# First stage of a four-stage graph kernel: the second bias of group 1 is summed on GpSimd, the gates of group 2 move up, more constant products on TensorE

## The chip, the cores and the metric

The kernel runs on one core of a Trainium2 chip. The metric is the device time of one execution in microseconds (us); lower is better. The engines are named as the profile does: PE (TensorE) with PEld (its weight loads), DVE (VectorE), ACT (ScalarE), POOL (GpSimd), SP (SyncE, which issues the DMAs).

## What is computed

`x` is 32 batches of 256 nodes with 128 features, `adj` a 256x256 matrix, all in float32. Four layers follow each other, each of them `x = layernorm(x + L(x))`. The change lies in the first:

```python
def _L0_gnn_ref(x, adj_in, adj_out, bias_in, bias_out, ...):
    msg_in = (einsum('nm,bmd->bnd', adj_in, x) + bias_in) * sigmoid(x @ gate_w_in + gate_b_in)
    msg_out = (einsum('nm,bmd->bnd', adj_out, x) + bias_out) * sigmoid(x @ gate_w_out + gate_b_out)
    msg_loop = x * sigmoid(x @ loop_gate)
    return relu(msg_in + msg_out + msg_loop)
```

Both adjacency matrices are the same `adj` here. With the gates g0, g1, g2 (one number per node and batch) the sum is `(adj x)(g0+g1) + bias_in g0 + bias_out g1 + x g2`. The later layers are a graph convolution with two batch norms, an attention layer, and a graph layer with ten LSTM steps; they are not touched.

## The kernel before

The 32 batches are worked on in `GROUPS` = 8 groups of `GB` = 4. A group is 8 tiles (`TILES`) of 128 nodes by 128 features, ordered as two halves (`NC` = 2) of four. Every engine has an instruction list of its own, written by hand, and the lists meet only in semaphores (`wait_ge`, `then_inc`), so the order of the statements in each engine's function is the order of its work.

The work of one group g in the first stage is this.

- PE: `gates(g)` (L574) gives the gates' sums, `neighbours(g)` (L582) gives `adj x`. Group 1 writes its neighbour sums to its own PSUM tile (named QQ in the profile), all others to PB. After the layer norm, `spread(g)` (L596) and `widen(g)` (L610) begin the second layer.
- DVE: `gate_sum(g)` (L1203) adds the gate biases. `gate_out(g)` (L1211 writes GG, L1213 writes GS = g0+g1) follows ACT's tanh. `mix(g)` makes the sum: eight L1284 (neighbour sum times GS, plus the tile V), eight L1291 (plus x times g2), for some groups one L1298 over all 1024 columns (plus the tile V2), one L1302 (relu, plus x), eight L1248 (statistics), then six small instructions L1260 to L1270 that end in the variance VAR.
- ACT: `squash(g)` (L940) is the tanh, `first_bias(g)` (L947) writes `V = bias_in g0` in eight instructions, `norm_apply` (L935) writes the normed tiles X.
- POOL: `second(g)` (L437) writes `V2 = bias_out g1` in two instructions, `both_biases(g)` (L446) adds V2 to V in two, and `rstd` (L413, L419) turns VAR into the scale RSD and the offset OFF for which `norm_apply` waits.

`APART` (L341) is the number of groups at the beginning whose V2 is added by DVE (L1298) and not by POOL (L446). It is 2 before: groups 0 and 1. In POOL's list `second(1)` stands behind `rstd(0, ...)` of group 0 and straight in front of `second(2)`. On PE, `spin(bank, count)` (L544) issues products of the constant tile `ones` whose results nobody reads: 8 of them before the first `neighbours(0)`, 10 before `spread(0)`.

Of the kernel before, what the change touches and what calls it, by code (L numbers as in the profile page):

```python
# [24 lines left out]
P = 128  # L25
BATCH, NODES, FEAT = 32, 256, 128
NC = NODES // P
GB = 4
# [62 lines left out]
def build(nc, x, xt, adj, early_in, later_in, lstm_w, out):  # L91
    ctx = ExitStack()
    with ctx:
# [6 lines left out]
        def reach(eng, s, n):  # L100

            if isinstance(n, int) and n <= 0:
                return
            eng.wait_ge(s, n)
# [94 lines left out]
        Q = [QQ[:, k * BANK:(k + 1) * BANK] for k in range(4)]  # L199
# [114 lines left out]
        def halves(g, h):  # L314
            return 2 * g + (2 if h is None else h + 1)

        def size(h):
            return 2 if h is None else 1
# [7 lines left out]
        def tls(h):  # L326
            return slice(0, TILES) if h is None else slice(h * TILES // 2, (h + 1) * TILES // 2)

        def nth(buf, t):
            return buf[:, t * P:(t + 1) * P]  # L330


        def near(g):
            return QA if g == 1 else PB
# [3 lines left out]
            return min(n, GROUPS)  # L338


        APART = 2  # L341


        NCHUNK, AHEAD = 2 * GROUPS, 3
# [55 lines left out]
        def _(pool):  # L400
# [7 lines left out]
            def rstd(k, kk, g, h=None):  # L408

                n, some = (halves(g, h), size(h)) if k in (1, 2) else (g + 1, 1)  # L410
                ts = tls(h)
                pool.wait_ge(ln[k]["var"], n)
                pool.tensor_tensor(RSD[kk][:, ts], VAR[kk][:, ts], pw[:, ts], ALU.pow).then_inc(ln[k]["rstd"], some)  # L413
                if k in (0, 1) or (k == 3 and g == GROUPS - 1):
                    pool.wait_ge(ln[k]["mean"], n)
                    pool.wait_ge(ln[k]["rstd"], n)
                    if k == 0:
                        reach(pool, ln[k]["out"], TILES * (g - 1))
                    pool.tensor_tensor(OFF[kk][:, ts], MEAN[kk][:, ts], RSD[kk][:, ts], ALU.mult).then_inc(ln[k]["off"], some)  # L419

            def wide(k):
                return BIO[:, k].unsqueeze(2).broadcast_to([P, NC, GB, P])

            def gate(g, k):
                return GG[g % 2][:, :, k:k + 1].rearrange("p (c b) q -> p c b q", c=NC).broadcast_to([P, NC, GB, P])

            def by_tile(buf):
                return buf.rearrange("p (c b d) -> p c b d", c=NC, b=GB)


            def second(g):

                pool.wait_ge(gate_g, g + 1)
                reach(pool, mix2, min(g - 1, APART))
                reach(pool, both_ok, NC * (g - 1 - APART))
                for c in range(NC):
                    pool.tensor_tensor(by_tile(V2[g % 2][:])[:, c:c + 1], wide(1)[:, c:c + 1], gate(g, 1)[:, c:c + 1],  # L437
                                       ALU.mult).then_inc(second_ok, 1)
# [13 lines left out]
            for c in range(NC):  # L452
                s = slice(c * P, (c + 1) * P)
                pool.wait_ge(norm_ok, NC + c + 1)
                pool.tensor_tensor(AN[:, c, s], AN[:, c, s], DIAG[:, c, :], ALU.add).then_inc(diag_ok, 1)
            rstd(0, 0, 0)
            second(1)
            for g in range(APART, GROUPS + 1):
                if g < GROUPS:
                    second(g)  # L460
# [79 lines left out]
        def _(pe):  # L540

            def spin(bank, count):
                for _ in range(count):
                    pe.matmul(bank, ones[:], ones[:], start=True, stop=True)  # L544
# [22 lines left out]
            def gates(g):  # L567
                pe.wait_ge(xt_in[g % NX], 16 * (g // NX + 1))
                if g == 0:
                    pe.wait_ge(early_ok, 16)  # L570
                reach(pe, gate_z, g)
                for c, b in ORDER:
                    at = (c * GB + b) * 4
                    mm = pe.matmul(Q[3][:, at:at + 4], turned(XT[:, g % NX], c, b), GW, start=True, stop=True)  # L574
                mm.then_inc(gate_ps, 1)
# [35 lines left out]
                              start=True, stop=True).then_inc(hid_ps, 1)  # L611

            pe.wait_ge(zero_ok, 1)
            spin(Q[0][:, 0:P], 8)
            pe.wait_ge(adjt_in, 16)
            neighbours(0)
            gates(0)
# [2 lines left out]
            neighbours(2)  # L620
            turn_adj()
            gates(2)
            spin(Q[2][:, 0:P], 10)
            for g in range(1, GROUPS + 1):
                spread(g - 1)
                if g + 2 < GROUPS:
# [163 lines left out]
            def lstm_x(g, par, k):  # L790

                p, s, _, nw = STEPS[k]
                if k == 0:
                    pe.wait_ge(h1_ok, 2 * (g + 1))
                    pe.wait_ge(z2_ok, TILES * 2) if g == 0 else None
                elif s == 0 and p > 1:
                    pe.wait_ge(h_ok, NSTEP * g + LAST_BEFORE[p] + 1)
                for q in gates_of(k):

                    before = max((j for (kk, qq), j in GATE_AT.items() if qq == q and kk < k), default=None)  # L800
                    last = max(j for (kk, qq), j in GATE_AT.items() if qq == q)
                    reach(pe, g_ok, NGATE * g + before + 1 if before is not None else NGATE * (g - 1) + last + 1)
                    mm = pe.matmul(steps_view(Q[q], k), WT[:, 0, (p - 1) * 4 + q, :], ht_view(par, k),  # L803
                                   start=True, stop=(s == 0))
                    if s == 0:
                        mm.then_inc(g_ps, 1)
# [382 lines left out]
        def _(dve):  # L1189
# [8 lines left out]
            def gate_sum(g):  # L1198
                dve.wait_ge(gate_ps, g + 1)
                if g == 0:  # L1200
                    dve.wait_ge(early_ok, 16)
                reach(dve, gate_t, g)
                dve.tensor_tensor(GZ[:].rearrange("p t q -> p (t q)"), Q[3][:, 0:TILES * 4],  # L1203
                                  GBI, ALU.add).then_inc(gate_z, 1)

            def gate_out(g):
                dve.wait_ge(gate_t, g + 1)
                reach(dve, first_ok, TILES * (g - 1))
                reach(dve, second_ok, NC * (g - 1))
                reach(dve, loop_ok, TILES * (g - 1))  # L1210
                dve.tensor_scalar(GG[g % 2][:], GT[:], 0.5, 0.5, ALU.mult, ALU.add).then_inc(gate_g, 1)  # L1211
                dve.wait_ge(gate_g, g + 1)
                dve.tensor_tensor(GS[g % 2][:], GG[g % 2][:, :, 0], GG[g % 2][:, :, 1], ALU.add).then_inc(gate_s, 1)  # L1213
# [36 lines left out]
            def norm_stats(k, kk, z, g, h=None):  # L1250

                norm_tiles(k, kk, z, g, h)
                norm_small(k, kk, g, h)
# [18 lines left out]
            def mix(g):  # L1272
                z = ZS[g % 2]
                if g == 1:
                    gate_sum(2)
                dve.wait_ge(gate_s, g + 1)
                dve.wait_ge(agg0_ps, g + 1)
                reach(dve, ln[0]["out"], TILES * (g - 1))
                for t in range(TILES):
                    if g < APART:  # L1280
                        dve.wait_ge(first_ok, TILES * g + t + 1)
                    elif t % GB == 0:
                        dve.wait_ge(both_ok, NC * (g - APART) + t // GB + 1)
                    dve.scalar_tensor_tensor(out=nth(z, t), in0=nth(near(g), t), scalar=GS[g % 2][:, t:t + 1],  # L1284
                                             in1=nth(V[g % 2], t), op0=ALU.mult, op1=ALU.add).then_inc(mix1, 1)
                if g == 1:
                    gate_out(2)
                dve.wait_ge(x_in[g % NX], 16 * (g // NX + 1))
                dve.wait_ge(mix1, TILES * (g + 1))
                for t in range(TILES):  # L1290
                    dve.scalar_tensor_tensor(out=nth(z, t), in0=nth(XIN[:, g % NX], t), scalar=GG[g % 2][:, t, 2:3],  # L1291
                                             in1=nth(z, t), op0=ALU.mult, op1=ALU.add).then_inc(loop_ok, 1)
                if g == 0:
                    gate_sum(1)
                dve.wait_ge(loop_ok, TILES * (g + 1))
                if g < APART:
                    dve.wait_ge(second_ok, NC * (g + 1))
                    dve.tensor_tensor(z[:], z[:], V2[g % 2][:], ALU.add).then_inc(mix2, 1)  # L1298
                    dve.wait_ge(mix2, g + 1)
                if g == 0:  # L1300
                    gate_out(1)
                dve.scalar_tensor_tensor(out=z[:], in0=z[:], scalar=0.0, in1=XIN[:, g % NX], op0=ALU.max,  # L1302
                                         op1=ALU.add).then_inc(mix3, 1)
                dve.wait_ge(mix3, g + 1)
                norm_stats(0, g % 2, z, g)
# [383 lines left out]
            g = GROUPS - 1  # L1689
# [53 lines left out]
```

## Time and profile before

| | us |
|---|---|
| three runs | 669.52, 670.06, 670.72 |
| their median | 670.06 |
| the profiled execution | 672.63 |
| its span on the core | 670.8 |
| busy in the span: PE, DVE, ACT, POOL | 635.3, 484.4, 426.6, 209.6 |

The span runs from the first to the last instruction in the trace, and 1.8 us of the profiled execution lie around it. The first stage, on which the change works, takes the first 110 us or so. Times of instructions below are counted from the start of the span. "<-" behind an idle time names what ended it.

### The profile page before, as it was taken

Reading aid. Unit: us, or ns where it says so; the run is one execution under the profiler, and the core shown is the slowest. Engines: PE = TensorE matmul, PEld = TensorE weight load, DVE = VectorE, ACT = ScalarE, POOL = GpSimd, SP = SyncE. Lnnn points to the kernel's source line nnn. Section 1 sums busy time; section 2 is a strip of 40 time slices with the busy share of each in tenths; the row PEclk is TensorE's granted clock in tenths of the full one; section 3 lists DMA queues with packets and bytes.
Section 4 is the critical chain, followed back from the end, with each engine's and each line's share of the span. In section 5 each row is a group of like instructions: output and inputs, shape, how many; then the busy total and the mean of one; then the engine's idle time right before and its main releaser. Section 6 shows DMA issues by size and latency. Waiting matters only on the chain.

```text
span 670.8 us, 9346 instructions
## 1 busy us (share of the span) xinstructions
PE 635.3 (95%) x2666; PEld 436.2 (65%) x2666; DVE 484.4 (72%) x1616; ACT 426.6 (64%) x953; POOL 209.6 (31%) x261
## 2 busy tenths in 40 slices
PE   9879999998899999999999999999999999999993
PEld 5745656446785687578657757765785686677573
DVE  3999999877856657876876787688668756465355
ACT  2656767866747665775667567656857666456562
POOL 2545451005724123234406132450522243012031
PEclk9989999998799999999999999999999999999998
DMA  8234000000000000000000000000000000000000
GB/s 330 108 110 173 1 1 1 1 0 1 0 1 1 0 1 0 1 0 33 1 0 19 13 1 0 33 1 0 1 31 1 0 33 0 1 1 32 1 32 31
DMA packets 4371, 16.82 MB, mean 25 GB/s; under 512 B 480, under 2 KB 480, under 8 KB 4192
## 3 DMA queue, kind: packets, MB, share of 16 engines
q1 hardware_dynamic: 4320, 16.23, 6.3%
q8 instruction: 21, 0.34, 0.2%
q14 instruction: 30, 0.25, 0.1%
HBM read 12.03 MB, written 4.19 MB: 24 GB/s over the span
## 4 chain that ended last, share of the span: by engine, by line
PE 63%; DVE 12%; ACT 6%; issue 3%; POOL 1%; DVEq 0%; ACTq 0%; POOLq 0%
PE QQ L803 22%; PE QQ L815 14%; PE PA L758 4%; PE PA L786 3%; PE PB L777 2%; PE PB L640 2%; PE PA L640 2%; DVE HT L1522 2%; ACT raw L1089 2%; ACT HB L1052 2%; DVE raw L1544 2%; PE PB L739 1%; PE PA L739 1%; PE PA L596 1%; ACT raw L1101 1%
## 5 line engine op out<-in xcount | busy, mean ns | idle before, releaser
L1089 ACT ACTIVATE raw<-QQ,BL 128x256 f32<-128x256 f32 (+4 forms) x312 | 166.6, 557 | 96.1 <-PE QQ L815 52.0
L803 PE MATMUL QQ<-HT,WT 128*128 128x256 f32 (+2 forms) x624 | 205.8, 473 | 6.7 <-ACT raw L1089 3.7
L803 PEld LDWEIGHTS QQ<-HT,WT 128*128 128x128 f32 x624 | 115.5, 190 | 73.9 <-issue 30.9
L413 POOL TENSOR_TENSOR RSD<-VAR,pw 128x8 f32<-128x8 f32 (+1 forms) x42 | 61.2, 1458 | 239.6 <-DVE VAR L1270 239.6
L815 PE MATMUL QQ<-HB,WT 128*128 128x256 f32 (+2 forms) x384 | 114.5, 441 | 2.0 <-DVE HB L1562 1.6
L815 PEld LDWEIGHTS QQ<-HB,WT 128*128 128x128 f32 x384 | 70.1, 190 | 36.1 <-issue 15.3
L500 POOL TENSOR_TENSOR HB<-HB 128x512 f32<-128x512 f32 x28 | 35.1, 1274 | 133.8 <-ACT HB L1042 133.8
L1101 ACT ACTIVATE raw<-raw 128x256 f32<-128x256 f32 (+4 forms) x88 | 41.5, 472 | 40.9 <-DVE raw L1544 32.5
L1534 DVE SCALAR_TENSOR_TENSOR raw<-raw 128x512 f32<-128x512 f32 (+2 forms) x66 | 39.4, 597 | 28.0 <-ACT raw L1089 27.4
L1562 DVE SCALAR_TENSOR_TENSOR HB<-raw 128x256 f32<-128x256 f32 (+4 forms) x48 | 21.8, 455 | 23.3 <-ACT raw L1101 23.3
L610 PE MATMUL QQ<-one_b,later 128*128 128x512 f32 x64 | 30.2, 613 | 4.7 <-ACT HB L974 4.5
L935 ACT ACTIVATE X<-Z,OFF,RSD 128x128 f32<-128x128 f32 x80 | 31.8, 481 | 2.0 <-POOL OFF L419 2.0
L481 POOL TENSOR_SCALAR X<-four,MEAN,RSD 128x128 f32<-128x128 f32 x64 | 32.4, 519 | 1.6
L596 PE MATMUL PA<-AHT,X 128*128 128x256 f32 x128 | 30.2, 390 | 1.9 <-ACT X L935 1.9
L1052 ACT ACTIVATE HB<-HB,EB 128x256 f32<-128x256 f32 x64 | 30.7, 495 | 1.6 <-POOL HB L500 1.5
L1562 DVE SCALAR_TENSOR_TENSOR HT<-raw 128x512 f32<-128x512 f32 (+4 forms) x40 | 21.7, 544 | 12.8 <-ACT raw L1101 12.4
L596 PEld LDWEIGHTS PA<-AHT,X 128*128 128x128 f32 x128 | 24.2, 194 | 10.2 <-issue 6.9
L758 PE MATMUL PA<-AD,X 128*128 128x256 f32 x128 | 30.5, 381 | 0.0
L786 PE MATMUL PA<-AD,Y 128*128 128x256 f32 x128 | 29.3, 381 | 0.0
L582 PE MATMUL PB<-four,AD 128*128 128x512 f32 x56 | 28.0, 647 | 0.6 <-DMA four<-in_x 0.6
L492 POOL TENSOR_SCALAR four<-HB,MEAN,RSD 128x128 f32<-128x128 f32 x56 | 28.1, 518 | 0.7
L758 PEld LDWEIGHTS PA<-AD,X 128*128 128x128 f32 x128 | 24.1, 193 | 6.4 <-issue 3.8
(223 smaller groups left out, 1101.0 us busy)
## 6 DMA issues: line engine op xcount, KB each, us to landing
four<-in_x SPq DMA_DIRECT2D x8, 512.0 KB, 3.7
raw<-in_xt SPq DMA_DIRECT2D x8, 512.0 KB, 6.4
out<-four SPq DMA_DIRECT2D x7, 512.0 KB, 2.7
WT<-in_lstm SPq DMA_DIRECT2D x1, 2048.0 KB, 9.3
later<-in_later SPq DMA_DIRECT2D x1, 725.5 KB, 10.0
AD<-in_adj SPq DMA_DIRECT2D x2, 256.0 KB, 4.9
out<-four SPq DMA_DIRECT2D x2, 256.0 KB, 2.0
early<-in_early SPq DMA_DIRECT2D x1, 275.0 KB, 4.4
```

The source lines that it names most:

```text
L413: pool.tensor_tensor(RSD[kk][:, ts], VAR[kk][:, ts], pw[:, ts], ALU.pow).then_inc(ln[k]["rstd"], some)
L500: pool.tensor_tensor(f.E1[:, 2 * b:2 * b + 2], f.E2[:, 2 * b:2 * b + 2], f.MS[:, 2 * b:2 * b + 2], ALU.add).then_inc(e_ok, 1)
L596: mm = pe.matmul(PA[:, b * NODES:(b + 1) * NODES], tile_of(X1, g, m, b), AHT[:, m, :], start=(m == 0), stop=(m == NC - 1))
L758: mm = pe.matmul(PA[:, b * NODES:(b + 1) * NODES], tile_of(X1, g, m, b), ADJT[:, m, :], start=(m == 0), stop=(m == NC - 1))
L786: mm = pe.matmul(PA[:, b * NODES:(b + 1) * NODES], turned(Y, m, b), ADJT[:, m, :], start=(m == 0), stop=(m == NC - 1))
L803: mm = pe.matmul(steps_view(Q[q], k), WT[:, 0, (p - 1) * 4 + q, :], ht_view(par, k), start=True, stop=(s == 0))
L815: pe.matmul(Q[q][:, 0:nw * GB], WT[:, 1, (p - 1) * 4 + q, :], HS[:, (k - 1) % 2, 0:nw * GB], start=False, stop=True).then_inc(g_ps, 1)
L1052: e = act.activation(f.E1[:, t], f.E1[:, t], ACT.Exp, bias=f.EB[:, t:t + 1], scale=SLOPE, accum_out=DEN[:, t:t + 1] if g > 1 else None)
L1089: act.activation(TG[q][:, at:n], Q[q][:, at:n], ACT.Tanh, scale=0.5 if q == G else 0.25, bias=BL[:, p - 1, q:q + 1]).then_inc(g_ok, 1)
L1101: act.activation(TC[:, at:n], CELL[:, at:n], ACT.Tanh, scale=0.5).then_inc(tc_ok, 1)
L1534: dve.scalar_tensor_tensor(out=target[:, 0:n], in0=TG[I][:, 0:n], scalar=1.0, in1=TG[G][:, 0:n], op0=ALU.add, op1=ALU.mult).then_inc(cell_ ...
L1562: dve.scalar_tensor_tensor(out=to[:, at:nw], in0=steps_view(TG[O], k)[:, at:nw], scalar=1.0, in1=steps_view(TC, k)[:, at:nw], op0=ALU.add, ...
```

## The change

```diff
-        APART = 2
+        APART = 1
...
@@ POOL's list
                 pool.wait_ge(norm_ok, NC + c + 1)
                 pool.tensor_tensor(AN[:, c, s], AN[:, c, s], DIAG[:, c, :], ALU.add).then_inc(diag_ok, 1)
-            rstd(0, 0, 0)
-            second(1)
             for g in range(APART, GROUPS + 1):
                 if g < GROUPS:
                     second(g)
                     both_biases(g)
                 rstd(0, (g - 1) % 2, g - 1)
...
@@ PE's list
             pe.wait_ge(zero_ok, 1)
-            spin(Q[0][:, 0:P], 8)
+            spin(Q[0][:, 0:P], 10)
...
             gates(2)
-            spin(Q[2][:, 0:P], 10)
+            spin(Q[2][:, 0:P], 20)
...
@@ DVE's mix(g)
                     dve.scalar_tensor_tensor(out=nth(z, t), in0=nth(near(g), t), scalar=GS[g % 2][:, t:t + 1],
                                              in1=nth(V[g % 2], t), op0=ALU.mult, op1=ALU.add).then_inc(mix1, 1)
-                if g == 1:
-                    gate_out(2)
+                    if (g, t) == (1, GB - 1):
+                        gate_out(2)
```

POOL's order at the beginning of the first stage, the difference between the two kernels. HT and Y are the two V2 tiles (group 1 has HT, group 2 has Y), one_a is V of group 1.

```order
 L455 TENSOR_TENSOR HB<-HB 128x128 [waits norm_ok] x2
+L437 TENSOR_TENSOR HT<-early,GG 128x512 [waits gate_g]
+L437 TENSOR_TENSOR HT<-early,GG 128x512
+L446 TENSOR_TENSOR one_a<-one_a,HT 128x512 [waits second_ok,first_ok] x2
 L413 TENSOR_TENSOR RSD<-VAR,pw 128x8 [waits ln0_var]
 L419 TENSOR_TENSOR OFF<-MEAN,RSD 128x8 [waits ln0_rstd,ln0_mean]
-L437 TENSOR_TENSOR HT<-early,GG 128x512 [waits gate_g]
-L437 TENSOR_TENSOR HT<-early,GG 128x512
 L437 TENSOR_TENSOR Y<-early,GG 128x512 [waits mix2,gate_g]
```

The two L437 of group 1 have moved in front of the L413 and L419 of group 0, and two L446 of group 1 are new behind them.

DVE's order in the mix of group 1, before:

```order
L1284 SCALAR_TENSOR_TENSOR X<-QQ,GS,one_a 128x128 [waits first_ok,agg0_ps,gate_s]
L1284 SCALAR_TENSOR_TENSOR X<-QQ,GS,one_a 128x128 [waits first_ok] x7
L1211 TENSOR_SCALAR GG<-GT 128x32 [waits second_ok,loop_ok,first_ok,gate_t]
L1213 TENSOR_TENSOR GS<-GG 128x8 [waits gate_g]
L1291 SCALAR_TENSOR_TENSOR X<-four,GG,X 128x128 [waits mix1,x_in1]
L1291 SCALAR_TENSOR_TENSOR X<-four,GG,X 128x128 x7
L1298 TENSOR_TENSOR X<-X,HT 128x1024 [waits second_ok,loop_ok]
L1302 SCALAR_TENSOR_TENSOR X<-X,four 128x1024 [waits mix2]
```

and now (the lines of the changed kernel are smaller by two from here on):

```order
L1282 SCALAR_TENSOR_TENSOR X<-QQ,GS,one_a 128x128 [waits both_ok,agg0_ps,gate_s]
L1282 SCALAR_TENSOR_TENSOR X<-QQ,GS,one_a 128x128 x3
L1209 TENSOR_SCALAR GG<-GT 128x32 [waits second_ok,loop_ok,first_ok,gate_t]
L1211 TENSOR_TENSOR GS<-GG 128x8 [waits gate_g]
L1282 SCALAR_TENSOR_TENSOR X<-QQ,GS,one_a 128x128 [waits both_ok]
L1282 SCALAR_TENSOR_TENSOR X<-QQ,GS,one_a 128x128 x3
L1289 SCALAR_TENSOR_TENSOR X<-four,GG,X 128x128 [waits mix1,x_in1]
L1289 SCALAR_TENSOR_TENSOR X<-four,GG,X 128x128 x7
L1300 SCALAR_TENSOR_TENSOR X<-X,four 128x1024 [waits loop_ok]
```

The 1024-column addition of V2 is gone, the first four and the last four sums now wait for POOL's `both_ok`, and the gates GG and GS of group 2 stand in the middle of the eight.

## Rows read from the trace of the kernel before

**Rows 1.** Busy time by stretch: us, busy (instructions) of each engine, PEclk, DMA share, GB/s

```profile
24.00:40.90 16.90, 10.66 (x60) 8.27 (x60) 16.24 (x46) 7.71 (x22) 9.64 (x9) 1.00 0.28 108
40.90:44.30 3.40, 3.19 (x5) 1.42 (x6) 3.30 (x11) 2.62 (x8) 2.83 (x4) 0.50 0.07 28
44.30:103.00 58.70, 58.55 (x222) 36.49 (x221) 56.73 (x185) 41.99 (x107) 29.98 (x28) 1.00 0.16 64
```

**Rows 2.** Waits of DVE and of PE from 24 to 110 us: total, times, longest

```profile
DVE Z L1284 <- DVE GS L1213: 0.4, 1, 0.4
DVE GG L1211 <- ACT GT L940: 0.3, 1, 0.3
...
PE QQ L610 <- ACT HB L974: 4.5, 1, 4.5
```

**Rows 3.** Timeline, PE at the start of spread(6): start, us busy, what, [idle before it]

```profile
103.00 3.69 PE L596 MATMUL PA<-AHT,X 128*128 128x256 f32 x16 [0.15 <-ACT X L935]
```

**Rows 4.** Timeline of DVE and POOL, the mix of group 1

```profile
24.63 0.17 DVE L1270 TENSOR_SCALAR VAR<-SQD 128x8 f32<-128x8 f32 x1
...
24.86 2.16 DVE L1284 SCALAR_TENSOR_TENSOR X<-QQ,GS,one_a 128x128 f32<-128x128 f32 x8
...
26.83 2.05 POOL L437 TENSOR_TENSOR HT<-early,GG 128x512 f32<-128x512 f32 x2
...
26.93 0.98 DVE L1211 TENSOR_SCALAR GG<-GT 128x32 f32<-128x32 f32 x1
...
28.84 5.86 DVE L1291 SCALAR_TENSOR_TENSOR X<-four,GG,X 128x128 f32<-128x128 f32 x8
28.84 2.10 POOL L437 TENSOR_TENSOR Y<-early,GG 128x512 f32<-128x512 f32 x2
...
31.34 2.68 POOL L446 TENSOR_TENSOR one_d<-one_d,Y 128x512 f32<-128x512 f32 x2 [0.40 <-ACT one_d L947]
...
34.73 1.22 DVE L1298 TENSOR_TENSOR X<-X,HT 128x1024 f32<-128x1024 f32 x1
...
39.62 0.17 DVE L1270 TENSOR_SCALAR VAR<-SQD 128x8 f32<-128x8 f32 x1
```

**Rows 5.** Timeline of DVE and POOL, the mix of group 3

```profile
53.29 2.16 DVE L1284 SCALAR_TENSOR_TENSOR X<-PB,GS,one_a 128x128 f32<-128x128 f32 x8
...
55.55 2.19 DVE L1291 SCALAR_TENSOR_TENSOR X<-four,GG,X 128x128 f32<-128x128 f32 x8
...
59.03 1.65 DVE L1248 BATCH_NORM_STATS2 STL<-X 128x6 f32<-128x128 f32 x8
...
60.15 2.52 POOL L446 TENSOR_TENSOR one_d<-one_d,Y 128x512 f32<-128x512 f32 x2 [4.95 <-ACT one_d L947]
60.71 0.74 DVE L1260 TENSOR_TENSOR SUM<-STL 128x16 f32<-128x16 f32 x1
...
61.57 1.13 DVE L1263 TENSOR_TENSOR SQD<-DIF 128x8 f32<-128x8 f32 x1
...
62.93 0.17 DVE L1270 TENSOR_SCALAR VAR<-SQD 128x8 f32<-128x8 f32 x1
```

**Rows 6.** Timeline of DVE and POOL, the end of group 0

```profile
20.70 0.18 DVE L1211 TENSOR_SCALAR GG<-GT 128x32 f32<-128x32 f32 x1
...
21.00 1.22 DVE L1302 SCALAR_TENSOR_TENSOR Z<-Z,four 128x1024 f32<-128x1024 f32 x1
...
24.88 1.65 POOL L413 TENSOR_TENSOR RSD<-VAR,pw 128x8 f32<-128x8 f32 x1 [6.41 <-DVE VAR L1270]
```

**Rows 7.** Timeline of PE and DVE, the first 17 us

```profile
1.03 3.78 PE L544 MATMUL QQ<-ones 128*128 128x128 f32 x16 [1.03 <-DVE ones L1215]
...
5.43 6.03 PE L582 MATMUL PB<-four,AD 128*128 128x512 f32 x8 [0.62 <-DMA four<-in_x]
...
13.00 3.68 PE L582 MATMUL QQ<-four,AD 128*128 128x512 f32 x8
...
13.18 0.19 DVE L1203 TENSOR_TENSOR GZ<-QQ,early 128x32 f32<-128x32 f32 x1 [3.03 <-PE QQ L574]
```

## The prediction

> **What bounds the kernel now.** I read the busy time by stretch first, then the waits, then the timeline of the groups around the change. The busy time [rows 1] shows two engines that are almost never idle in the first stage: from 24.0 to 40.9 us DVE is busy for 16.24 of 16.90 us while PE works only 10.66; from 44.3 to 103.0 DVE is busy for 56.73 of 58.70 us and PE for 58.55. The waits [rows 2] say the same: between 24 and 110 us DVE waits twice, for 0.3 and 0.4 us. PE has one long wait in that stretch, 4.5 us for ACT in widen(0), and ACT there is itself waiting for a gate sum that DVE issues late. So the first stage goes at DVE's pace, with PE just behind. At spread(6) the two meet: PE waits 0.15 us for a normed tile [rows 3], which comes out of DVE's variance. Whatever DVE gains before 103 us moves the rest of the program, if PE follows; the later stages are untouched.
>
> DVE's "busy" is not all work. Eight L1291 take 2.19 us in group 3 [rows 5] and 5.86 us in group 1 [rows 4]; GG takes 0.98 us in group 1 and 0.18 in the group before [rows 6]. In group 1 POOL's L437, L437 and L446 (2.05, 2.10 and 2.68 us) run just beside these. L1284 (2.16 us in both groups) and L1248 (1.65) do not stretch beside POOL: L437 starts at 26.83 while L1284 ends, and L446 at 60.15 runs beside L1248. The Trainium skill (SBUF — State Buffer, "Who interferes with whom") has the rule: a DVE instruction with two SBUF inputs contends with a GpSimd instruction that reads SBUF, and the second one to come blocks fully. By that rule the trace agrees: L1291, L1298, L1302 and the small L1260 to L1267 mostly have two such inputs, L1284 and L1248 have one. The change is therefore mostly about which DVE instruction stands beside POOL's.
>
> **Part 1: group 0 gets slower.** POOL's four instructions of group 1 now start when GG of group 1 is ready, 20.88 us (20.70 + 0.18) [rows 6], in what was an idle time of 6.41 us in front of L413. They are 2.05 us (two L437, rows 4) and 2.52 us (two L446, rows 5), together 4.6 us. Beside them DVE has L1302, which starts at 21.00, the eight L1248, and the small ones. Either L1302 is held behind the first L437, by about what GG lost in group 1, 0.98 - 0.18 = 0.8 us, or it goes first and POOL's four end that much later. The L446 meet the small ones as in group 3, where L1260 took 0.74 and L1263 1.13 us [rows 5]; undisturbed ones take 0.17, so that costs 1.5 us. Together the variance of group 0 comes **2.3 us later**. Bounds: 0, if every piece of POOL's falls beside L1248 or waits, and 4.6 us, if all of it stops DVE. I take 2.3, since group 3 shows the same L446 pair at the same place. POOL's four are through by then (20.9 + 4.6 = 25.5, or some 26.7 if L1302 goes first, against a variance at 26.9), so L413, and the new wait of L1284 for both_ok, cost nothing more; the cover for that is a few tenths. What is queued behind the new wait for first_ok on POOL is L413 itself, and ACT's first bias of group 1 starts at the same GG, so it keeps ahead.
>
> **Part 2: the mix of group 1 gets faster.** Before, it takes from L1284 at 24.86 to VAR at 39.62, 14.76 us [rows 4]. The new one is made from group 3 [rows 5], which has no L1298 either: 5.74 us from L1284 to L1248 (53.29 to 59.03), 1.68 to L1260, and from L1260 to VAR 2.22 less the 1.5 us of blocking, 0.7. That is 8.1 us. GG and GS in the middle of the L1284 add 0.4, but no longer meet an L437: those wait for GG and for L419 of group 0. L437 starts 1.97 us after the first L1284 (26.83 against 24.86), and that distance stays, since both hang on VAR of group 0; the pair then ends 4.0 us after it. L1291 begins at 2.26 + 0.4 = 2.7, so it is held for about 1.2 us. Before, two pairs stood there, HT and Y; now only Y. The L446 of group 2 hang on ACT's first bias and would start 31.34 - 24.86 = 6.5 us after the first L1284. DVE is then in L1302 (6.1 plus the 1.2 of blocking, less the 1.2 it takes, to 8.5 at the latest), so POOL is the one held, or L1302 is; L1248 shields DVE after that, and the end of the second L446 costs the small ones 0.8. Sum: 8.1 + 0.4 + 1.2 + 0.8 = 10.5 us, **4.3 us less than 14.76**. It contains the L1298 removed (1.22 us) and the rest is blocking that goes. Less the 2.3 of part 1, DVE is ahead by **2.0 us** after group 1. With the bounds of part 1 that term lies between -0.3 and +4.3.
>
> From group 2 on the lists are as before, and hang on the same chain. PE has to follow: spread(1) hangs on VAR of group 1 and so moves with it. PE also loses less to its clock. Before, its 4.5 us wait is followed by a stretch from 40.9 to 44.3 us with a granted clock of 0.5, the 1.2 GHz level [rows 1, 2]; now widen(0) has its ACT copy about 2 us earlier, while spread(0) ends 2.3 us later, so the gap shrinks to nearly nothing, and a matmul stream that ran at 1.2 GHz for part of those 3.4 us may run at 2.4. That puts PE ahead of DVE and not behind, so I count nothing for it. The twelve extra products cost PE: ten of them, at half of the 0.47 us (3.78 / 8) that one takes in the first stretch [rows 7], 2.4 us. They fill the 2.3 us by which the normed tiles of group 0 are late, and behind them PE has that 4.5 us wait as a reserve. Nothing.
>
> **Part 3: the first products.** At the start PE's four neighbour products of group 0 take 6.03 us, those of group 1 3.68 [rows 7]. It is the same work: the first ran mostly at 1.2 GHz, the second at 2.4. Before the first, PE had been busy from 1.03 to 4.81 and idle for 0.62. DVE's first gate sum waits for PE at 13.18, so this is on the path. Two more products are 0.9 us and close the gap; then PE is busy without a break from 1.03 instead of 5.43, and the clock can rise before or in the neighbour products. Bounds: 6.03 - 3.68 = 2.35 us if they run wholly at 2.4 GHz; 0.3 us lost (0.9 - 0.6) if the rise comes where it came before and the extra products are in the way. I take **2.0 us**, near the upper end, because the break is the only thing between two busy stretches and 4.4 us of busy time are added in front. The Trainium skill (TensorE: Matmul & The Clock Gate, Part 1) says that the place of the rise varies between runs of the same kernel, with where the first matmul falls. By that rule this term would be an average and could not be read from one trace; the three runs before spread over 1.2 us, which would fit. No trace here shows it.
>
> **Sum.** 2.0 + 2.0 = 4.0 us off the profiled execution's 672.63. The median of the runs is 670.06, 2.6 us lower; I take the same saving from it: **666.1 us**. A measurement of this kernel can tell about 0.2%, 1.3 us, from no change.
>
> **The rivals.**
> - The forecast, both terms as above: 666.1. Chance 0.48.
> - The clock does not rise earlier. For it: between 1.03 and 4.81 PE was already busy and the level did not change. Only part 1 and 2 count: 670.06 - 2.0 = 668.1. Chance 0.21.
> - POOL blocks DVE in full in group 0 (4.6 us instead of 2.3), and only the clock helps: 670.06 + 0.3 - 2.0 = 668.4. For it: in group 1 three pairs of POOL's cost DVE 3.7 us in L1291 (5.86 - 2.19) and 0.8 in GG [rows 4], most of their length. Against it: 1.65 us of DVE's time there is L1248. Chance 0.09.
> - Neither helps, or the one eats the other; that is also the case in which the change does not do what it says: 669.7 to 670.4. Chance 0.13.
> - Slower: L446 comes to stand beside L1291. In group 1 that cost about 2 us (of the 3.7 in L1291), in group 3 the same L446 costs 1.5 beside L1260 to L1263, and where it meets only one small one less than 1. If the normed tiles and the first biases of ACT come earlier against DVE in groups 3 to 7, by more than the 1.1 us between the start of L1248 and of L446 (59.03 and 60.15) plus L1302's 1.2, then each of the five groups pays about 1 us more: +5.0 - 2.0 = 3.0 over, 673.1 without the clock's help. Against it: ACT's first bias hangs on PE, and PE gains at most the 1.7 us of the slow clock over DVE. Chance 0.09.
>
> **How the numbers follow.** Faster by over 0.2% are the first three, 0.78; within 0.2% the fourth, 0.13; slower 0.09. The range goes from 663.4, where part 1 costs 0.5 and the clock gives 2.3 (4.3 - 0.5 + 2.35 is 6.2; 663.9, and some tenths for PE's clock), to 669.0, beyond the second and third cases.
>
> **What the profile would show.** Right: L1302 and the small instructions of group 0 stretched, VAR of group 0 some 2.3 us later against its gate sum; no L1298 in group 1, L1291 there near 3.4 us and no longer 5.86; GG of group 2 near 0.18; L1284 to VAR in group 1 near 10.5; PE's wait in widen(0) gone and no 0.5 clock around 41 us; the neighbour products of group 0 near 3.9 us and the first gate sum near 11.2. Wrong, if the first gate sum still comes at 13.2, if L1284 of group 1 waits for both_ok, or if PE starts to wait for ACT in groups 3 to 7.

## The result, and the profile after

The changed kernel takes 664.18 us (median of five runs, 662.84 to 665.25) against 670.06 us (five runs, 668.51 to 673.05): a ratio of 0.9908, 95% interval 0.9885 to 0.9931. That is 5.9 us less, where 4.0 were forecast, and it lies inside the range.

The profiled executions differ by more, 661.2 against 670.8 us of span. To see why, the trace needs one marker in the middle. The start of spread(6), the matmul group that waited for DVE in [rows 3], serves well: it is near the end of the first stage, and behind it the two programs are the same.

The timeline of the changed kernel, PE and DVE at the start (its lines are smaller by two; start, us busy, what), against [rows 7]:

```profile
1.03 4.52 PE L542 MATMUL QQ<-ones 128*128 128x128 f32 x20 [1.03 <-DVE ones L1213]
...
5.47 3.67 PE L580 MATMUL PB<-four,AD 128*128 128x512 f32 x8
...
10.86 0.19 DVE L1201 TENSOR_TENSOR GZ<-QQ,early 128x32 f32<-128x32 f32 x1 [1.58 <-PE QQ L572]
```

The four neighbour products of group 0 take 3.67 us in place of 6.03, and the first gate sum comes at 10.86 instead of 13.18. Which clock level such a short stretch had is read here from the durations, since the granted-clock column shows 1.00 at the start of both traces, while the same four products take 6.03 or 3.67 us. Where the rise falls can be read too: the instructions of the constant products start 0.21 us apart before it and 0.11 us behind it, those of the neighbour products take 1.06 and then 0.59 us. In the kernel before it comes at 10.2 us, in the changed one at 5.3.

The same view, the end of group 0 on DVE and POOL, against [rows 6]:

```profile
18.64 3.04 POOL L437 TENSOR_TENSOR HT<-early,GG 128x512 f32<-128x512 f32 x2 [2.49 <-DVE GG L1209]
18.68 2.08 DVE L1300 SCALAR_TENSOR_TENSOR Z<-Z,four 128x1024 f32<-128x1024 f32 x1
...
21.64 2.51 POOL L446 TENSOR_TENSOR one_a<-one_a,HT 128x512 f32<-128x512 f32 x2
22.48 0.45 DVE L1258 TENSOR_TENSOR SUM<-STL 128x16 f32<-128x16 f32 x1
...
23.05 1.13 DVE L1261 TENSOR_TENSOR SQD<-DIF 128x8 f32<-128x8 f32 x1
...
24.41 0.17 DVE L1268 TENSOR_SCALAR VAR<-SQD 128x8 f32<-128x8 f32 x1
```

L437 and L1300 start 0.04 us apart and hold each other: L1300 takes 2.08 us for 1.22, and the two L437 take 3.04 for 2.05, since the second is held while L1300 runs. The L446 then hold L1258 and L1261.

And the mix of group 1, against [rows 4]:

```profile
24.64 1.13 DVE L1282 SCALAR_TENSOR_TENSOR X<-QQ,GS,one_a 128x128 f32<-128x128 f32 x4
...
25.68 0.17 DVE L1209 TENSOR_SCALAR GG<-GT 128x32 f32<-128x32 f32 x1
...
26.62 2.10 POOL L437 TENSOR_TENSOR Y<-early,GG 128x512 f32<-128x512 f32 x2
...
27.20 3.24 DVE L1289 SCALAR_TENSOR_TENSOR X<-four,GG,X 128x128 f32<-128x128 f32 x8
...
30.48 1.23 DVE L1300 SCALAR_TENSOR_TENSOR X<-X,four 128x1024 f32<-128x1024 f32 x1
...
31.12 2.94 POOL L446 TENSOR_TENSOR one_d<-one_d,Y 128x512 f32<-128x512 f32 x2 [2.40 <-ACT one_d L945]
...
34.61 0.17 DVE L1268 TENSOR_SCALAR VAR<-SQD 128x8 f32<-128x8 f32 x1
```

L1289 takes 3.24 us in place of 5.86, GG 0.17 in place of 0.98, L1298 is gone, and the L446 of group 2 now meet L1300, where POOL is the one that waits (2.94 us in place of 2.52). The last two rows are PE at spread(1) and spread(6), against [rows 3]:

```profile
37.91 3.69 PE L594 MATMUL PA<-AHT,X 128*128 128x256 f32 x16 [0.97 <-ACT X L933]
...
97.30 3.69 PE L594 MATMUL PA<-AHT,X 128*128 128x256 f32 x16 [0.15 <-ACT X L933]
```

spread(6) starts at 97.30 against 103.00, 5.7 us earlier. So the first stage carries what the medians show. The other 3.9 us of the two spans come later, 2.6 of them by 224 us, behind the stretch of the attention stage where the clock differs. Busy time by stretch, the kernel before (the column behind the five engines is the granted clock; 1.00 is 2.4 GHz and 0.50 is 1.2 GHz):

```profile
163.80:177.40 13.60, 11.47 (x78) 9.02 (x77) 11.92 (x57) 12.13 (x30) 8.02 (x7) 1.00 0.00 1
177.40:184.30 6.90, 6.31 (x29) 5.86 (x28) 4.81 (x21) 3.96 (x10) 5.31 (x7) 0.51 0.00 0
```

and the changed kernel:

```profile
155.00:158.40 3.40, 3.40 (x10) 1.74 (x9) 1.47 (x8) 3.40 (x10) 3.26 (x4) 0.57 0.00 0
158.40:653.00 494.60, 479.56 (x2098) 340.18 (x2096) 342.81 (x1175) 320.26 (x712) 150.04 (x192) 1.00 0.02 8
```

Each trace has one fall of 3.4 us near 155 to 160 us. The trace of before has 6.9 us more at the 1.2 GHz level from 177.4 on, the other none. The length of that second fall differs from one execution of the same kernel to the next, as the repeated traces below show, and a version of the changed kernel has it too (`after_10_10`, 6.8 us at a granted clock of 0.50 from 172.3 on). So I don't count it as the change's work. It is not shown that the change has no part in it: the fall is in all three traces of the kernel before.

### The profile page after: what moved, and what is told of

Its sections match the earlier page's. It is cut to its first block, busy times and chain, and to the rows that moved or that the text cites. A ratio compares the mean times of both kernels' runs of the same rounds, so it can differ in the third digit from the quotient of the medians.

```text
span 661.2 us, 9396 instructions
## 1 busy us (share of the span) xinstructions
PE 630.9 (95%) x2690; PEld 434.8 (66%) x2690; DVE 481.7 (73%) x1615; ACT 426.9 (65%) x953; POOL 214.4 (32%) x263
## 4 chain that ended last, share of the span: by engine, by line
PE 64%; DVE 11%; ACT 6%; issue 3%; POOL 1%; DVEq 0%; ACTq 0%; POOLq 0%
PE QQ L801 23%; PE QQ L813 14%; PE PA L756 4%; PE PA L784 4%; PE PB L775 2%; PE PB L638 2%; PE PA L638 2%; DVE HT L1520 2%; ACT HB L1050 2%; ACT raw L1087 2%; DVE raw L1542 1%; PE PB L737 1%; PE PB L823 1%; PE PA L737 1%; DVE HB L1435 1%
## 5 line engine op out<-in xcount | busy, mean ns | idle before, releaser
L413 POOL TENSOR_TENSOR RSD<-VAR,pw 128x8 f32<-128x8 f32 (+1 forms) x42 | 61.7, 1470 | 223.9 <-DVE VAR L1268 223.9
L784 PEld LDWEIGHTS PA<-AD,Y 128*128 128x128 f32 x128 | 24.2, 190 | 5.0 <-DVE Y L1513 0.7
```

The source lines that it names most:

```text
L784: mm = pe.matmul(PA[:, b * NODES:(b + 1) * NODES], turned(Y, m, b), ADJT[:, m, :], start=(m == 0), stop=(m == NC - 1))
```

## The experiments

In the table below, "gate sum" is the start of DVE's first GZ and "spread(6)" the start of PE's eight products of that group, both from the timeline of each profiled execution. Times are in us. Each is a median, and the ratio is to runs of the kernel before on the same chip (its medians there were 669.97, 669.83, 668.97 and 669.86 us). Two versions that ran on different chips are compared best by their ratios; 0.001 is 0.67 us.

| kernel | time | ratio, interval | neighbours(0) | gate sum | spread(6) | from one to the other |
|---|---|---|---|---|---|---|
| before | 670.06 | | 6.03 | 13.18 | 103.00 | 89.82 |
| changed | 664.18 | 0.9908, 0.9885 to 0.9931 | 3.67 | 10.86 | 97.30 | 86.44 |
| sum_only | 664.99 | 0.9934, 0.9909 to 0.9959 | 5.63 | 13.10 | 99.76 | 86.66 |
| first_products | 668.55 | 0.9982, 0.9969 to 0.9995 | 3.67 | 11.72 | 102.55 | 90.83 |
| after_10_10 | 664.96 | 0.9923, 0.9903 to 0.9944 | 3.67 | 11.24 | 97.93 | 86.69 |
| gates_behind | 664.48 | 0.9924, 0.9907 to 0.9942 | 3.67 | 11.34 | 98.14 | 86.80 |
| short_sums | 662.90 | 0.9907, 0.9877 to 0.9938 | 3.67 | 11.27 | 96.45 | 85.18 |
| sum_8_20 | 665.18 | 0.9938, 0.9916 to 0.9960 | 3.67 | 11.11 | 97.56 | 86.45 |
| first_14 | 664.86 | 0.9922, 0.9898 to 0.9946 | 3.60 | 11.88 | 98.50 | 86.62 |
| later_products | 664.17 | 0.9919, 0.9894 to 0.9943 | 4.02 | 11.66 | 98.10 | 86.44 |
| no_first | 664.79 | 0.9935, 0.9912 to 0.9958 | 5.75 | 13.28 | 99.74 | 86.46 |
| before, second trace (one run) | 671.13 | | 5.82 | 13.37 | 103.09 | 89.72 |
| before, third trace (one run) | 668.91 | | 3.67 | 11.24 | 103.02 | 91.78 |
| wait_filled_pa | 666.86 | 0.9952, 0.9936 to 0.9969 | 3.67 | 11.31 | 100.47 | 89.16 |

### The two halves of the change, apart

`sum_only` is the changed kernel with the constant products of before:

```diff
-            spin(Q[0][:, 0:P], 10)
+            spin(Q[0][:, 0:P], 8)
...
-            spin(Q[2][:, 0:P], 20)
+            spin(Q[2][:, 0:P], 10)
```

> The changed kernel with 8 and 10 constant products, as before: only the sum on GpSimd and the moved gates. Theory (two separate terms): the first gate sum comes near 13.2 us again, the variance of group 1 near 37.0 (2.6 earlier than 39.62), and the time is about 2.5 to 3.4 us under before, 667.1. Rival (the products are all of it, and what group 1 gains is lost to group 0): within 1 us of before, 670.

`first_products` is the kernel before with the two more first products:

```diff
-            spin(Q[0][:, 0:P], 8)
+            spin(Q[0][:, 0:P], 10)
```

> The kernel before with 10 first constant products in place of 8 and nothing else. Theory (the break in front of the first neighbour products holds the clock down): neighbour products of group 0 in 3.7 us and not 6.0, first gate sum near 10.9, time 2.3 us under before, 667.8. Rival (the rise came early in the changed kernel by the luck of that run): first gate sum at 11 to 14 us, time within 1 us of before, 670.

In `sum_only` the variance of group 1 comes at 36.84 (forecast 37.0) and spread(6) 3.24 us before that of the kernel before. The time is 5.0 us lower, more than expected, but the interval (0.9909 to 0.9959, 2.7 to 6.1 us) takes in both; the experiments below give a reason for the size. The rival falls: the sum on GpSimd is a gain by itself.

`first_products` splits its theory. The neighbour products are fast (3.67 us) and the gate sum comes 1.46 us earlier, but spread(6) only 0.45, and the time falls by 1.4 us (interval 0.3 to 2.1 us). The early start is there and then mostly gone. Its timeline of PE shows where:

```profile
39.31 2.04 PE L610 MATMUL QQ<-one_b,later 128*128 128x512 f32 x2 [4.48 <-ACT HB L974]
...
41.45 5.48 PE L596 MATMUL PA<-AHT,X 128*128 128x256 f32 x16
```

spread(1) takes 5.48 us, where its sixteen instructions take 3.69 at 2.4 GHz. It stands behind the 4.48 us wait in widen(0), and the clock is down there from 38.3 to 45.1 us:

```profile
38.30:45.10 6.80, 5.70 (x11) 3.46 (x12) 6.31 (x21) 5.88 (x16) 3.86 (x4) 0.50 0.21 85
```

In the kernel before this stretch of half clock is 3.4 us long [rows 1].

### Is that a matter of the single run?

> The kernel before, unchanged, for a second trace. Theory (the place of the clock's rise varies from run to run with 8 first products): the neighbour products of group 0 take anything from 3.7 to 6.0 us, and the fall in widen(0) comes somewhere between 37 and 45 us or not. Rival (the break always holds the clock down here): 5.6 to 6.0 us again, as in two of three traces with 8 products.

> The kernel before, unchanged, for a third trace. Same theories as for the second trace: another duration of the first neighbour products, between 3.7 and 6.0 us, or 5.6 to 6.0 each time.

The theory holds. The second trace of the unchanged kernel has neighbour products of 5.82 us, the third 3.67. So with 8 products the early rise comes by itself in some executions (`sum_8_20` is another). It came in the third trace although PE stood idle for 1.04 us in front of the neighbour products, longer than the 0.62 us of the first trace [rows 7], where it did not come:

```profile
5.85 3.67 PE L582 MATMUL PB<-four,AD 128*128 128x512 f32 x8 [1.04 <-DMA four<-in_x]
```

The third trace also answers the question of `first_products` best. Its PE at the wait:

```profile
38.84 1.21 PE L610 MATMUL QQ<-one_b,later 128*128 128x512 f32 x2 [4.49 <-ACT HB L974]
40.98 6.42 PE L596 MATMUL PA<-AHT,X 128*128 128x256 f32 x16 [0.93 <-ACT X L935]
47.24 1.84 PE L574 MATMUL QQ<-early,raw 128*128 128x4 f32 x16
48.95 3.68 PE L582 MATMUL PB<-four,AD 128*128 128x512 f32 x8
```

and its busy time by stretch:

```profile
39.70:46.50 6.80, 5.87 (x14) 4.47 (x14) 6.63 (x21) 6.48 (x18) 3.37 (x4) 0.50 0.05 7
```

spread(1) starts 1.9 us earlier than in the first trace and takes 6.42 us, because it is wholly at 1.2 GHz (granted clock 0.50 from 39.7 to 46.5). It ends within 0.1 us of where it ends in the first trace, and spread(6) starts at 103.02, as in the other two (103.00 and 103.09). All that the early rise brought was paid back at the long wait. That this comes out so evenly belongs to these traces: in `first_products` the fall is 6.8 us long as well, but it begins 3.1 us before spread(1), and 0.45 us are left.

The two repeats also show that the later fall varies. The second trace is at half clock for half of the 6.9 us of the first:

```profile
177.40:180.80 3.40, 2.92 (x14) 2.52 (x13) 2.38 (x11) 3.10 (x8) 2.79 (x6) 0.50 0.00 0
180.80:184.30 3.50, 3.50 (x25) 3.25 (x25) 3.04 (x16) 0.94 (x3) 2.53 (x3) 1.00 0.00 0
```

### The wait filled

`wait_filled_pa` leaves the sum on DVE and keeps the clock up through the wait:

```diff
-            spin(Q[0][:, 0:P], 8)
+            spin(Q[0][:, 0:P], 10)
...
                     n = 4 * g + r
+                    if n == 3:
+                        spin(PA[:, 0:P], 17)
                     reach(pe, hid_ok, n - 2)
```

> The kernel before with 10 first products and 17 more constant products in front of the last product of widen(0), where PE waits 4.5 us; the sum of group 1 stays on DVE. Theory (with the long wait left idle the clock falls behind it and gives the early start back, as in the traces with the early rise): no half clock near 40 us, spread(1) in 3.7 us, the stage behind runs 2.3 to 3.0 us earlier, time 2.3 to 3.0 us under before, 667. Rival (the early start is lost to something else, such as DVE's own pace or the copies of x): the neighbour products of group 3 near 48.5 us again as in the traces of before, time as with 10 first products alone, 668.5.

The theory holds. Its PE:

```profile
34.28 3.96 PE L544 MATMUL PA<-ones 128*128 128x128 f32 x34
38.84 1.12 PE L612 MATMUL QQ<-one_b,later 128*128 128x512 f32 x2 [0.60 <-ACT HB L976]
41.07 3.69 PE L596 MATMUL PA<-AHT,X 128*128 128x256 f32 x16 [1.11 <-ACT X L937]
...
46.30 3.68 PE L582 MATMUL PB<-four,AD 128*128 128x512 f32 x8
```

and its busy time from 30 to 60 us, with no fall of the granted clock:

```profile
30.00:60.00 30.00, 28.11 (x139) 20.11 (x140) 28.92 (x87) 18.78 (x47) 14.85 (x14) 1.00 0.26 93
```

The neighbour products of group 3 start at 46.30 instead of 48.95, spread(6) at 100.47, and the time is 666.86 us, 3.0 under before and 1.7 under `first_products`. The execution in the trace is one of the longest of its twelve (669.74, of 665.42 to 669.83): it has later falls, 3.4 us from 157.9 and 6.8 us from 174.9 on, like the first trace of before. So the change's two halves depend on each other: the sum on GpSimd removes the wait that makes the early clock worthless. That also fits the 5.0 us of `sum_only`. Its trace has the late rise and is 3.2 us ahead at spread(6); the trace of `sum_8_20`, again with 8 first products, has the early rise and is 5.4 ahead. With the wait gone, an early rise that comes by itself is kept. The medians alone would not have told this: 1.4 and 5.0 us add up to 6.4, near the 5.9 of both.

### The first products in the changed kernel

```diff
-            spin(Q[0][:, 0:P], 10)
+            spin(Q[0][:, 0:P], 8)
```

> The changed kernel with 8 first products in place of 10. Theory (the first two products are worth in the changed kernel what they are worth alone, less what clock falls give back): first gate sum near 13.1, 1.4 to 2.3 us over the changed kernel, 665.6 to 666.5. Rival (with the long wait in widen(0) gone the clock has no second place to fall, so they are worth the full 2.3): 666.5.

`no_first` has 1 there, `first_14` has 14.

> The changed kernel with one first product in place of ten. Theory (the products serve to have the clock up before the neighbour products): these take 5.5 to 7.0 us, first gate sum 12.8 to 14.5, time 1.5 to 3.3 us over the changed kernel, 665.7 to 667.5. Rival (PE's own neighbour products set the rise and 8 or 10 in front change little): within 1 us of 664.2.

> The changed kernel with 14 first products. Theory (once the clock is up, more of them only stand in front of the neighbour products): neighbour products start at 6.1 to 6.9 us and not at 5.5 to 5.9, time 0.3 to 1.0 us over the changed kernel, 664.5 to 665.2. Rival (the copy of x lands at up to 6.3 us in some runs and the longer filling keeps the clock up in more of them): 0.5 us under, 663.7.

With one product the neighbour products take 5.75 us and the gate sum comes 2.42 us later than in the changed kernel. spread(6) comes 2.44 later: now nothing is given back. With 8 the one trace has the early rise, so the expected 13.1 was missed, and the median is 1.0 us higher, within the spread of both. From 10 on, eight traces of eight had neighbour products of 3.60 to 4.02 us; with 8, two of five. So what the two products can buy is that the early rise comes more often, and not a fixed time. Even that is likely and not proven. In `first_products` and `wait_filled_pa` the rise came at 4.1 and 4.3 us, before the two added products had begun (at 4.4), so those two traces would have had it with 8 as well; six of six against two of five are left. The trace that speaks most for the products is `later_products`: its rise comes at 6.6 us, where the traces with 8 have 5.3, 5.6, 9.7, 10.2 and 10.2.

The medians are milder than the traces: `no_first` was expected 1.5 to 3.3 us over the changed kernel and is 0.6 over (four runs, 663.75 to 666.11, the profiled one 666.11), `sum_only` and `sum_8_20`, with the same 8 first products, 0.8 and 1.0. By the ratios, which leave the chip out, the three are 1.8, 1.7 and 2.0 us over. The intervals of all of them overlap with that of the changed kernel, so how much the first products bring on average there is not settled beyond "0.6 to 2.0 us". With 14 the neighbour products start at 6.56, where the other versions of the changed kernel have 5.47 to 5.95; that is 1.0 us at the gate sum against the changed kernel's trace and 0.7 in the medians, again within the intervals.

### The second products, and the gates in the middle

`after_10_10`:

```diff
-            spin(Q[2][:, 0:P], 20)
+            spin(Q[2][:, 0:P], 10)
```

> The changed kernel with 10 and 10 constant products. Theory (the ten extra ones in front of spread(0) fill a wait and cost and bring nothing): same time as the changed kernel, 664.2, within 0.7. Rival (they keep the clock up through the wait for group 0's tiles): a stretch at half clock near 26 to 30 us comes back, and the time is 0.7 to 1.7 us over the changed kernel, 665 to 666.

The fall comes: spread(0) starts at 28.11 after 3.69 us of waiting and takes 5.38 us.

```profile
28.11 5.38 PE L594 MATMUL PA<-AHT,X 128*128 128x256 f32 x16 [3.69 <-ACT X L933]
...
38.54 3.68 PE L594 MATMUL PA<-AHT,X 128*128 128x256 f32 x16
```

But from the gate sum to spread(6) it is only 0.25 us longer than in the changed kernel: what hangs on spread(0) has room. The median is 0.8 us higher, 1.0 by the ratio, within both intervals. The ten products are worth a few tenths in the first stage by this trace, and the times can't tell it from nothing.

`gates_behind`:

```diff
-                    if (g, t) == (1, GB - 1):
+                    if (g, t) == (1, TILES - 1):
                         gate_out(2)
```

> The changed kernel with the gates of group 2 behind all eight sums of group 1 instead of behind the fourth. Theory (GpSimd's L437 starts only after L419, at 26.5 us, so the gates need not be ready before): L437 starts some 0.4 us later, the variance of group 1 within 0.4 us, same time, 664.2. Rival (the gates run into L437 again as before the change and are held 0.8 us each): GG and GS near 1 us each, time 1 to 1.6 us over the changed kernel, 665.2 to 665.8.

GG takes 0.17 us here too, at 27.21, and L437 starts at 27.46, having waited 0.3 us for it. All of it now stands beside L1289, which takes 3.78 us in place of 3.24. The variance of group 1 comes 10.32 us after the first L1282, against 9.97. GG would thus not have been held at the end either; the place of the gates is worth 0.35 us, under what the medians can tell. Here GG began before L437; in the kernel before it began 0.10 us behind it (26.93 against 26.83) [rows 4] and was held for 0.8 us. GG reads one tensor only, so the prediction's division into instructions with one input and with two does not cover it.

### What holds DVE

`short_sums`:

```diff
+                    s = slice(s.start, s.start + 8) if g == 1 else s
                     pool.tensor_tensor(V[g % 2][:, s], V[g % 2][:, s], V2[g % 2][:, s], ALU.add).then_inc(both_ok, 1)
```

> The changed kernel, but POOL's two L446 of group 1 add only the first 8 of 512 columns (most of bias_out times g1 of group 1 is left out of the result). Theory (L446 holds DVE's small two-input instructions): L1258 and L1261 of group 0 near 0.17 and not 0.45 and 1.13, the variance of group 0 1.2 to 1.3 us earlier against its gate sum, L1300 still 2.1 us (that is L437's doing), time 1.2 us under the changed kernel, 663.0. Rival (what comes before the small ones sets them, the wait for their statistics or for a semaphore): they stay at 0.45 and 1.13 and the time stays at 664.2.

Its DVE and POOL (the lines are one larger):

```profile
19.05 3.03 POOL L437 TENSOR_TENSOR HT<-early,GG 128x512 f32<-128x512 f32 x2 [2.49 <-DVE GG L1210]
19.09 2.08 DVE L1301 SCALAR_TENSOR_TENSOR Z<-Z,four 128x1024 f32<-128x1024 f32 x1
...
22.05 0.38 POOL L447 TENSOR_TENSOR one_a<-one_a,HT 128x8 f32<-128x8 f32 x2
22.89 0.17 DVE L1259 TENSOR_TENSOR SUM<-STL 128x16 f32<-128x16 f32 x1
...
23.18 0.17 DVE L1262 TENSOR_TENSOR SQD<-DIF 128x8 f32<-128x8 f32 x1
```

The small instructions are back at 0.17 us, L1301 is still 2.08, and from the gate sum to spread(6) 1.26 us go, as expected. The statistics are unchanged, so the rival falls: the stretching of DVE's small instructions in group 0 is L446's doing. The gain shows in the trace alone. The median is 1.3 us under the changed kernel's, but the ratio is the same (0.9907 against 0.9908), and the four runs lie from 661.97 to 665.70.

### Products in front of the attention stage

```diff
-            spin(QB[:, 0:P], 4)
+            spin(QB[:, 0:P], 12)
```

> The changed kernel with 12 instead of 4 constant products in front of the first transposes of the attention stage, near 150 us, where PE then idles 1.4 and 0.9 us. Theory (the clock falls there or behind in some runs, 3.4 us at half clock near 155 in the changed kernel's trace, and the products prevent it): no half clock near 155, 0.5 to 1.7 us under the changed kernel, 662.5 to 663.7. Rival (the falls there come from the gaps further on, and the products stand in front of the transposes): same or up to 0.5 us slower, 664.2 to 664.7.

The trace has no fall near 155 us, but the median is that of the changed kernel (664.17). Other traces without these products have no fall there either (`short_sums`, `sum_only`), so one trace settles nothing, and the time says that they bring nothing that can be measured. No version here beats the changed kernel by more than the spread, not even `short_sums`, which leaves work out.

## Why the prediction was right

By its own steps, each against the trace of the changed kernel:

- **What bounds.** DVE sets the pace through groups 0 and 1, as read. Behind them the reading was wrong in both traces: spread(2) to spread(5) start exactly 12.17 us apart in the kernel before (55.79 to 92.30) and in the changed one (50.09 to 86.60), and PE takes the normed tiles late. From VAR to spread(g) it is 3.3 us where PE waits for the tiles (groups 0, 1 and 6), but 4.8 to 5.5 us in groups 2 to 5. That DVE is busy for 56.73 of 58.70 us there does not make it the engine that bounds.
- **Part 1**, group 0 slower by 2.3 us: measured 2.10 (gate sum to variance 13.55 us against 11.45). L1300 lost 0.86 (0.8 forecast), and L1258 to VAR takes 1.93 us, 1.2 more than the 0.7 of undisturbed ones (1.5 forecast).
- **Part 2**, the mix of group 1 in 10.5 us for 14.76: measured 9.97, so 4.8 saved and not 4.3. L1289 was forecast near 3.4 and is 3.24. The L446 of group 2 came while L1300 ran and POOL waited, one of the two orders that the step left open; L1258 then loses 0.5 us and not 0.8.
- **The net term** is therefore 2.7 us after group 1 where 2.0 were forecast.
- **"I count nothing for it"** is the step that failed in kind: PE's clock behind the wait. From VAR of group 1 to spread(6) the kernel before takes 63.4 us and the changed one 62.7. PE is busy without a break from spread(1) to spread(6) in both, so what the half clock costs it there (4.38 us for spread(1) in the timeline, 3.69 now) comes out at the end. `wait_filled_pa` shows the same 0.7 by itself: 89.16 us from gate sum to spread(6) against 89.82, with the sum still on DVE. The step took PE's saving for a lead over a DVE that sets the pace, but behind spread(1) PE was the later of the two. The term was put at nothing and measured 0.7.
- **Part 3**, 2.0 us: 2.32 in the profiled pair. That this one pair comes near the forecast is in part luck: the kernel before had the late rise in two traces of three, and the changed trace has the earliest gate sum of all (10.86, where its versions with 10 first products have 11.24 to 11.66). The reason given, that the break is the only thing between two busy stretches, does not hold: the early rise came across breaks of 0.91 us (`sum_8_20`) and 1.04 us (the third trace of before), both longer than the 0.62 that were to be closed. What decides was not found. That the place of the rise varies is now shown: 10.2, 10.2 and 5.6 us in three traces of one kernel. The Trainium skill (TensorE: Matmul & The Clock Gate, Part 1) says that it varies between runs of the same kernel, which no trace had shown when the prediction was made, and the traces agree.
- **The sum** of the three in the trace is 2.7 + 0.7 + 2.3 = 5.7 us, and the medians differ by 5.9. The prediction added two terms as if they were independent. They are not: in the traces the first products alone bring 0.45 us at spread(6), the sum alone 3.2, both 5.7. The 5.7 are at the upper end. The versions with 10 first products whose first stage is nearly the changed kernel's (`after_10_10`, `gates_behind`, `later_products`) start spread(6) at 97.93 to 98.14, 4.9 to 5.1 us before the kernel before. The forecast of 4.0 us less thus came from a first term 0.7 too small, a clock term of 0.7 left out, and a last one that is right in size for a reason that failed.

The rivals: the clock did rise earlier; POOL did not block in full (2.1 us in group 0, not 4.6); and L446 did not come to stand beside L1289 in groups 3 to 7, where it starts beside the statistics as before. That last one was not tried by a run of its own.

Open is a drift of about 1 us between the two traces in the later stages (from 8.3 us apart near 223 us to 9.4 near 590). It appears in some pairs of traces of one kernel too and was not followed up.

## What to carry to other kernels

When two engines block each other on shared access, work out what stands beside what: moving GpSimd's work out from beside a stream of two-input instructions (L1291) was worth more than the removed instruction itself. The mix of group 1 lost 4.8 us, of which 1.2 are L1298; 2.1 of it came back as a cost in group 0, where the moved work now holds L1300 and the small instructions. A gain at the start of a stage is only worth what the next long wait leaves of it, so test the parts of a change alone and together, and look at a marker in the middle of the trace rather than at the span. Take a second trace of the unchanged kernel before you price a clock effect from one.

## What was not expected of the hardware

- Three traces of one unchanged kernel put its first matmuls at 6.03, 5.82 and 3.67 us and still started spread(6) within 0.09 us of each other. The trace with the early rise had 6.8 us at half clock around the 4.5 us wait and behind it (39.7 to 46.5), the others 3.4 (40.9 to 44.3): the later fall undid the earlier rise almost exactly.
- When L437 and L1300 start 0.04 us apart, both are held in turn: DVE first waits 0.86 us for the first L437, then the second L437 waits about 1 us for L1300. An instruction pair on GpSimd does not keep DVE out for its whole length. The Trainium skill (SBUF — State Buffer, "Who interferes with whom") states the exclusive lock for the whole instruction, and the trace agrees instruction by instruction.
